# Preparing steps of a two-stage language-model tower: rows transposed ahead, one power, weight split moved into the attention, first block maxima taken early

## What is computed

```
h = h + attn(layernorm(h))                 # first stage, untouched by the change
x = layernorm(h)                           # eps 1e-5
hx = layernorm(x) * ln_g + ln_b            # a second layernorm of the same rows
q, k, v = hx @ Wq, hx @ Wk, hx @ Wv        # 2 heads of 64, 2 x 2048 rows
q, k = l2norm(q) * 8 * qn_g, l2norm(k) * 8 * kn_g
attn = softmax(where(causal, q @ k.T / 8, min))
y = (attn @ v) @ Wo
gate = softmax(y @ gate_W + gate_b)        # 8 experts
out = sum_e gate_e * (gelu(y @ W1_e + b1_e) @ W2_e + b2_e)
h = h + out
```

## Time and profile before

| | us |
|---|---|
| median of three timed runs | 964.7 (964.68 to 965.3) |
| the profiled execution | 964.4 |
| its span in the trace | 962.3 |
| PE busy | 827.2 (86%) |
| DVE busy | 732.0 (76%) |
| ACT busy | 513.4 (53%) |
| POOL busy | 366.6 (38%) |

### The profile page before, as it was taken

One profiled execution on the slowest core, in us unless ns is written; L12 is line 12 of the kernel. 1 busy time (PEld: TensorE's weight loads), 2 busy tenths in 40 slices (PEclk: granted clock), 3 DMA queues, 4 the chain that ended last, 5 costly groups with the idle time before them and its releaser, 6 DMA issues.

```text
span 962.3 us, 21449 instructions
## 1 busy us (share of the span) xinstructions
PE 827.2 (86%) x7864; PEld 592.4 (62%) x7864; DVE 732.0 (76%) x1725; ACT 513.4 (53%) x1069; POOL 366.6 (38%) x478
## 2 busy tenths in 40 slices
PE   1677999999667565888898998699999999999997
PEld 1555777777433333556665666477777777777775
DVE  5736666666579896667667774399999999999997
ACT  1322444444056765667686898455555555555553
POOL 7565555555567774455565676100000000000000
PEclk9887999999656766899999999799999999999999
DMA  3110000000001110000000000000000000000000
GB/s 124 46 26 4 1 0 0 0 0 0 1 22 43 33 41 16 1 1 2 2 2 1 2 2 2 1 2 13 2 12 2 13 3 11 13 2 13 2 13 12
DMA packets 9474, 11.65 MB, mean 12 GB/s; under 512 B 1832, under 2 KB 6704, under 8 KB 9264
## 3 DMA queue, kind: packets, MB, share of 16 engines
q1 hardware_dynamic: 8368, 8.43, 2.9%
q0 software_dynamic: 1024, 2.10, 0.8%
HBM read 8.43 MB, written 2.10 MB: 11 GB/s over the span
## 4 chain that ended last, share of the span: by engine, by line
PE 60%; DVE 11%; POOL 11%; issue 9%; ACT 7%; DMA 0%; DVEq 0%; POOLq 0%; ACTq 0%
PE ps L897 59%; POOL plo L359 3%; DVE mx L794 2%; DVE y L684 2%; ACT phi L520 2%; POOL h_all L221 2%; ACT p L519 1%; POOL rr L306 1%; POOL rr L315 1%; DVE x L726 1%; DVE ss L732 1%; POOL ss L323 1%; ACT ql L506 1%; ACT arena L408 1%; PE ps L1167 0%
## 5 line engine op out<-in xcount | busy, mean ns | idle before, releaser
L897 PE MATMUL ps<-y,arena 128*128 128x512 f16 (+1 forms) x896 | 247.4, 424 | 19.3 <-DVE y L684 17.0
L548 ACT ACTIVATE cst<-ps,col 128x512 f32<-128x512 f32 x256 | 176.1, 688 | 163.6 <-PE ps L897 163.6
L897 PEld LDWEIGHTS ps<-arena,sq 128*128 128x128 f16 x3072 | 192.8, 98 | 60.5 <-DVE sq L883 0.7
L897 PE MATMUL ps<-arena,sq 128*128 128x128 f16 x3072 | 213.0, 219 | 0.5 <-DVE sq L883 0.5
L883 DVE TENSOR_TENSOR sq<-cst,sq 128x512 f16<-128x512 f32 x256 | 175.7, 686 | 4.4
L359 POOL TENSOR_TENSOR plo<-p,phi 128x512 f16<-128x512 f32 (+2 forms) x120 | 124.8, 1058 | 89.8 <-ACT phi L520 88.2
L878 DVE CAST sq<-cst 128x512 f16<-128x512 f32 x256 | 108.0, 422 | 12.2 <-ACT cst L548 3.1
L897 PEld LDWEIGHTS ps<-y,arena 128*128 128x128 f16 (+1 forms) x896 | 75.4, 112 | 58.5 <-issue 24.8
L794 DVE TENSOR_REDUCE mx<-ps 128x1 f32<-128x512 f32 (+3 forms) x160 | 91.3, 604 | 24.6 <-PE ps L897 23.8
L519 ACT ACTIVATE p<-ps 128x512 f32<-128x512 f32 (+3 forms) x160 | 88.2, 552 | 23.8 <-PE ps L897 22.6
L520 ACT ACTIVATE phi<-ps 128x512 f16<-128x512 f32 (+3 forms) x160 | 88.7, 554 | 0.0
(11 more groups left out here) (153 smaller groups left out, 1305.8 us busy)
## 6 DMA issues: line engine op xcount, KB each, us to landing
sq<-w_rows SPq DMA_DIRECT2D x16, 256.0 KB, 2.7
out<-h_all SPq DMA_DIRECT2D x32, 64.0 KB, 1.6
cst<-consts SPq DMA_DIRECT2D x1, 1294.0 KB
h_all<-emb_rows,idx POOLq DMA_INDIRECT x32
wqkv<-w_qkv SPq DMA_DIRECT2D x1, 192.0 KB
wsm<-w_sm SPq DMA_DIRECT2D x1, 192.0 KB
row<-rows SPq DMA_DIRECT2D x1, 140.0 KB
c<-consts SPq DMA_DIRECT2D x1, 96.0 KB
```

Of the source, the lines that this page charges most:

```text
L548: a.activation(hid[:, f], ps[:, HBANK[f], :], ACT.Gelu_apprx_tanh, bias=col[:, K_B1 + k:K_B1 + k + 1], scale=1.0 / WS).then_inc(S["hid_rea ...
L897: return t_.matmul(o, l, r, start=start, stop=stop, skip_group_check=True)
```

## The change

It has four parts.

**Order of the preparing step.** In `step_a2` the transposes of the rows of chunk c+2 (PE) now stand ahead of the transposes of q and k of chunk c. On ACT `normed_T(c + 2)` likewise stands ahead of `high_qk(c)`.

**One power.** The factor of the two layernorms is taken as one power of var·(1+eps)+eps². DVE makes that number in a new step `two_norms`, at the end of `low_qk`, and POOL has one operation in the place of seven.

**The weights.** The 16 pieces are no longer split in the preparing stage but in the softmax attention, one piece for each eight steps k. ACT writes the high part after the exponentials of k = 6, 14, ... 126 (one operation, the scaled copy is gone), DVE the low part at k+4 with one `scalar_tensor_tensor`. SP loads a piece once the piece two before it is done.

**The first item's maxima.** Its four blocks are scored and reduced in the last four preparing steps, PE at the start of each and DVE at the end of each, all in PSUM bank 7. PE waits in each for DVE's reduce of the step before.

```diff
 # SP
-            with sp.Fori(2, NT - 1, 2) as n:
...
+            for n in range(2, NPIECE):
+                sp.wait_ge(S["wlow_ready"], n - 1)
+                sp.dma_start(stage[n % 2], w12_rows[:, n * 512:(n + 1) * 512]).then_inc(S[STAGED[n % 2]], 16)
 # POOL
             def both_norms(c, par):
                 pool.wait_ge(S["stats2"], c + 1)
...
+                g.tensor_tensor(rr[par][:, 1], rr[par][:, 0], mhalf[:, 0:B], ALU.pow).then_inc(S["rr_ready"], 1)
 # ACT
+            def weights_high(n):
+                act.wait_ge(S[STAGED[n % 2]], 16 * (n // 2 + 1))
+                a.activation(w12[:, 4 * n:4 * n + 4, 0, :], stage[n % 2].rearrange("p (w d) -> p w d", d=D),
+                             ACT.Copy, scale=WS).then_inc(S["whigh_ready"], 1)
...
             def step_a2(c, par, left=3):
                 if left >= 1:
                     squares(c + 1, 1 - par)
-                high_qk(c)
                 if left >= 2:
                     normed_T(c + 2, par)
-                weights_high(c, par)
+                high_qk(c)
...
+                    if k in WSLOT:
+                        weights_high(WSLOT.index(k))
 # DVE
+            def two_norms(c, par):
+                dve.wait_ge(S["agg2"], c + 1)
+                v.tensor_scalar(rr[par][:, 0], mv2[par][:, :, 1], 1.0 + LN_EPS, LN_EPS * LN_EPS, ALU.mult, ALU.add
+                                ).then_inc(S["stats2"], 1)
...
                 low_qk(c)
+                if left >= 3:
+                    two_norms(c + 3, 1 - par)
                 if left >= 1:
                     low_v(c + 1, 1 - par)
...
+                row_max(0, MPARTS[0][c - NT + 4])
...
+            def weights_low(n):
+                piece = w12[:, 4 * n:4 * n + 4]
+                dve.wait_ge(S["whigh_ready"], n + 1)
+                v.scalar_tensor_tensor(piece[:, :, 1, :], stage[n % 2].rearrange("p (w d) -> p w d", d=D), WS,
+                                       piece[:, :, 0, :], ALU.mult, ALU.subtract).then_inc(S["wlow_ready"], 1)
...
+                if k - 4 in WSLOT:
+                    weights_low(WSLOT.index(k - 4))
 # PE
+                if 0 < k < 4:
+                    pe.wait_ge(S["sm_used"], k)
...
             def step_a2(c, par, left=3):
                 if left >= 1:
                     project2(c + 1, 1 - par)
-                unit_T(c)
                 if left >= 2:
                     normed_T(c + 2, par)
+                unit_T(c)
...
+                max_scores(0, MPARTS[0][c - NT + 4])
                 step_a2(c, c % 2, NT - 1 - c)
...
+WSLOT = [8 * n + 6 for n in range(2 * E * FF // 512)]
+
+
+def max_bank(k):
+    return 7 if k < 4 else (2, 3, 5)[k % 3]
```

More of the change, by code:

```diff
@@ L129, in tower @@
         mv2 = [sb(f"mv2{i}", [P, B, 2]) for i in range(2)]
-        rr = [sb(f"rr{i}", [P, 4, B]) for i in range(2)]
+        rr = [sb(f"rr{i}", [P, 2, B]) for i in range(2)]
         x2 = [sb(f"x2{i}", [P, B, D]) for i in range(2)]
@@ L348, in _ @@
                     step_a2(c + u, u)
-            for c in range(NT - 4, NT):
+            for c in range(NT - 4, NT - 1):
                 step_a2(c, c % 2, NT - 1 - c)
@@ L770, in _, with row_max @@
             low_v(0, 0)
+            def row_max(it, part):
+                r, kb, w, k = part
+                dve.wait_ge(S["sm_ps"], k + 1)
+                v.tensor_reduce(mx[:, r, kb:kb + 1], ps[:, max_bank(k), 0:w], AX, ALU.max).then_inc(S["sm_used"], 1)
+                c, _, h = ITEMS[it]
+                if (r, kb) == (3, c):
+                    dve.wait_ge(S["sm_used"], k + 1)
+                    v.tensor_reduce(mall[:], mx[:, :, 0:c + 1], AX, ALU.max).then_inc(S["max_link"], 1)
+                    dve.wait_ge(S["max_link"], it + 1)
+                    if it >= HS:
+                        dve.wait_ge(S["mrow_ps"], it - 1)
+                    v.tensor_scalar(mpad[:, h, :, DS], mall[:], -1.0, None, ALU.mult).then_inc(S["mneg"], 1)
             def step_a2(c, par, left=3):
@@ L1055, in _, with max_scores @@
             normed_T(1, 1)
+            def max_scores(it, part):
+                c, b, h = ITEMS[it]
+                r, kb, w, k = part
+                q = b * N + c * CH + r * P
+                if 0 < k < 4:
+                    pe.wait_ge(S["sm_used"], k)
+                elif k >= 7:
+                    pe.wait_ge(S["sm_used"], k - 2)
+                last = mm(ps[:, max_bank(k), 0:w], qhh[:, h, q:q + P], khl[:, h, b * N + kb * CH:b * N + kb * CH + w],
+                          stop=kb < c)
+                if kb == c:
+                    last = mm(ps[:, max_bank(k), w - P:w], ident16, neg_qk, start=False)
+                last.then_inc(S["sm_ps"], 1)
             def step_a2(c, par, left=3):
@@ L1067, in _ @@
             for c in range(NT - 4, NT):
+                if c == NT - 4:
+                    pe.wait_ge(S["hi_ready"], 8)
+                    pe.wait_ge(S["lo_ready"], 1 + 8)
+                max_scores(0, MPARTS[0][c - NT + 4])
                 step_a2(c, c % 2, NT - 1 - c)
@@ L1127, in values @@
                 last.then_inc(S["pv_done"], 1)
-            for part in MPARTS[0]:
-                max_scores(0, part)
             max_row(0)
```

80 lines of the change are left out of this document (12 added, 68 removed).

## The result

The changed kernel took 977.09 us (median of 4 runs, 976.56 to 977.57) against 964.69 for the kernel before on the same chip: a ratio of 1.0128, 95% interval 1.0111 to 1.0146. The prediction was 974.5 us, slower. Its profiled execution took 977.57 us with a span of 975.8; before it was 964.4 and 962.3.

The account below looks back on a forecast made before the run. No engine is full in the preparing stage; a circle of waits through POOL and DVE sets its step. 964.4 + 6.8 for the stage + 3.3 for the weights in the attention = 974.5 us, range 963 to 985.

Parts of the forecast that it names:

- Part 1: Preparing loop: one power cuts the POOL and DVE circle to 4.05 us; step about 6 if nothing else late.
- The stage's start: Start of the preparing stage: fewer POOL operations ahead of the first attention's last factors, -0.4 us (0 to -1.0).
- Part 2: Preparing loop: the new order makes each step one serial row, 7.00 to 7.70 us; twelve steps cost +4.2 us.
- rival A: Preparing loop: the new order costs nothing, steps about 6.0 us, kernel 959 us; chance 12%.
- The signs that I gave: Preparing loop: scalings 7.0 to 7.7 us apart, DVE idle before low parts, ACT before its first high part.
- Part 3: Last preparing steps: early maxima cost +0.8 us in chunk 12, +4.0 in chunks 13 and 14; the end gains -1.8.
- Chunk 12's step: Near the preparing stage's end: one added DVE reduce, 7.6 us against 6.82, +0.8 (+0.5 to +1.2).
- Part 4: Softmax attention: splitting the weights there costs ACT and DVE together +3.3 us, from 0 to 17.0.
- ACT's term: Softmax attention: 16 high-part operations, ten places of 0.58 us without a gap, 30% felt by PE: 1.7 us.
- DVE's term: Softmax attention: 16 low-part operations of 0.7 us, mostly covered by idle time before `plo`, 15% of 11.2: 1.7 us.
- Rival C: Softmax attention: none of the weight work is covered, +17.0 us, kernel 988 us; sign over 8 us longer; chance 10%.
- Rival B: Whole kernel: high clock level throughout, stage +0.1, weights hidden at 0 to 3, about 965.5 us; chance 15%.

Follow-up runs that it names:

- e4: The kernel before with the one power alone; order, weights and first maxima as before: 954.07 us, ratio 0.9937 to the kernel before.
- e10: The kernel before, unedited, run again for its trace on another chip: 960.14 us, ratio 0.9976.
- e5: The changed kernel, unedited, run again on another chip: 975.92 us, ratio 1.0154 to the kernel before.
- e1: The changed kernel with only the old order of transposes and high parts put back: 972.74 us, ratio 1.0133 to the kernel before.
- e3: The changed kernel with the first item's four maxima back behind the preparing stage: 971.99 us, ratio 1.0110 to the kernel before.
- e8: The changed kernel without DVE's operation on the weights, low halves set to zero by POOL: 967.91 us, ratio 1.0081 to the kernel before.
- e12: The kernel before with the one power and the early maxima, PE's block behind its step's work: 955.43 us, ratio 0.9918 to the kernel before.

## Why the prediction was right, point by point

**The total** was right (974.5 against 977.1), and so were the sign and the range. Its closeness was luck: the stage was forecast 4.0 us too long and the attention 6.1 too short. The changed kernel's trace adds 2.2 us ahead of the stage and takes 0.8 from the experts, both outside the change: over all 14 traces the start of the stage lay between 251.8 and 255.9 us, whatever the kernel.

**Part 1** was right in that the circle goes, and its step was too short. I called for "about 6" us a step if nothing else were late; with the power alone the steps were 6.4 to 6.5. I had put x2 at 0.60 because POOL's operation for the weights leaves the stage; e4 has x2 at 0.67 with that operation still there, so the one power had brought this too, and moving the weights was not needed for it. The stage's start gained 1.5 us against the first trace and 0.7 against e10's, where I had -0.4, at most -1.0.

**Part 2, the order**, had the mechanism right, and rival A (steps of about 6, 959 us) is excluded. The term was mis-sized: +4.2, measured +1.1 (e5's loop even lies 1.0 below e10's). A step took 6.82 us with the transposes at the high level and 7.48 to 7.50 with them at the low one, where I had summed 7.00 and 7.70. The 0.2 is what lies between the start of the x2 transposes and ACT's first high part, 1.01 instead of 0.44 + 0.79; my other terms miss by about 0.1 each and nearly cancel. I had put two groups of matmuls end to end that overlap. And the transposes stood at the high level in 8 of 12 steps, where I had taken half. That makes a mean of 7.04 instead of 7.3. I had read the share of steps off a share of the time, and the two differ: the granted clock over the loop was 0.71, two fifths of the time at the high level, but the product runs mostly at the low level, beside the row of work, where it costs nothing. The signs that I gave fit with two exceptions: most scalings stand 6.82 apart and not 7.0 or more, and ACT's idle time stands before `hxT`, not before its first high part. The error that mattered was in the reading of the term, not in its size. I costed the order against the old step of 6.95; against the step that the one power allows (6.46 in e1), it costs 7.04 - 6.46 = 0.6 us a step, 7 us in all (5 by e5's loop).

**Part 3, the maxima**: -1.7 for the end against -1.8, and +4.9 for chunks 13 and 14 against +4.0, by the wait that I had named. The size of the +4.9 is partly luck: the two steps ran almost wholly at the low level, for which I had summed 18.2 us, and took 17.0; I had discounted for the high level instead. Chunk 12's step took 6.82 us in both kernels (forecast +0.8); it was 6.64 in e3, so the reduce costs about 0.2 there, and the 7.6 that I had put for the step was too long by what part 2 was.

**Part 4, the weights**, is the step that failed. ACT's term was 1.7 and measured 2.0; its factor of 30% was a guess, and no run shows how its delays pass on. No piece waited for its load (ACT idled 0.2 us before all of them). DVE's term was 1.7 and measured 6.0, 0.38 us for each piece of 0.965 us. I had 0.7 us a piece and 15% of it uncovered, and argued from DVE's idle time before its own `plo`. Two things were wrong with that. First, the piece stands ahead of block maxima too, and PE's loads for the next block wait for those: 12.0 us of waits instead of 3.2, back to 3.4 in e8. Of the 12.0 us, 10.9 stand in the 5 us behind the start of a piece. The place was in the order that I showed ahead of the prediction, where the row at L800 stands ahead of two reduces for `mx`; I costed only the `plo` behind it. Second, the operations stretch each other. My 0.7 us was right for a piece by itself (0.68); the mean of 0.965 comes from those that met a POOL operation. The Trainium skill ("SBUF — State Buffer", section "Who interferes with whom") says that DVE and GpSimd hold one pair of ports against each other, as an exclusive lock. The trace agrees, by the rows at 480.56 and 529.70; x2, which I had named for it, has one input tensor and says less of an operation with two. By that rule I had the cost of the 16 nearer to the upper end, 11.2, than to my 1.7; the 6.0 lie about halfway. `plo` took 47 ns more on POOL (114 of them, 5.4 us) and 128 ns more on DVE (39, 5.0 us), and both went back when the piece was left out. How the 6.0 us divide between the place and the stretching is open; a piece at another place was not tried. Rival C (nothing covered, +17.0) is excluded: 9.7 us on ACT and 15.4 on DVE were added in this window, and 8.0 came out. The attention did grow by 9.4 us, past the 8 that I had given as a sign of C, so that sign could not tell C from a mis-sized forecast.

**Rival B** is excluded by the attention, though its stage (+0.1) was closer to the measured +2.8 than mine (+6.8).

## What to carry to other kernels

A change of several parts should be run part by part: here one of four parts (one power instead of two and six small operations) gains 6 to 8 us (0.6% and 0.9%) by itself, and the three others take more than that back. When a bound is removed together with a reorder, cost the reorder against the step that would be left without it, not against the old step; and when a wait is put ahead of an engine's work, count what is queued behind it and put it behind that work instead, as e12 did. Work moved into another engine's idle time must be costed against every consumer behind its place in the queue, not only against the operation that the idle time was read from.
